# Start of a GRU with an expert layer: load requests on one queue, and two blocks of x turned in steps 0 and 1

## What is computed

```
gi = x_t @ W_ih + b_ih                     # 512 -> 3*512
gh = h @ W_hh + b_hh
r = sigmoid(i_r + h_r); z = sigmoid(i_z + h_z)
n = tanh(i_n + r * h_n)
h = (1 - z) * n + z * h                    # 256 such steps, one after the other

logits = h / |h| @ router_w                # top 2 of 8, weights normalized
out = x + sum_e combine[:, e] * (h @ Wa[e] @ Wb[e])
```

## Time and profile before

| | us |
|---|---|
| median of 3 runs | 1015.8 |
| lowest, highest | 1015.31, 1016.97 |
| the profiled execution | 1016.61 |
| its span in the profile | 1014.8 |
| granted TensorE clock, mean of the span | 0.998 |

### The profile page before, as it was taken

The page is one execution under the profiler, slowest core; times in us unless marked ns, Lnnn a source line. Parts: engine busy times, 40 slices in busy tenths (PEclk is TensorE's granted clock), DMA queues, the critical chain, the costliest instruction groups (busy, mean ns, idle before and its releaser), DMA issues.

```text
span 1014.8 us, 60727 instructions
## 1 busy us (share of the span) xinstructions
PE 979.8 (97%) x29067; PEld 669.7 (66%) x20799; DVE 877.1 (86%) x3637; ACT 695.7 (69%) x2696; POOL 292.5 (29%) x723
## 2 busy tenths in 40 slices
PE   4789999999999999999999999999999999999997
PEld 2456666666666667766666666666676677676674
DVE  6889888888888888888888888888888888888887
ACT  6687766776766776666677676677666667766664
POOL 1032233232333332323332332332332332233223
PEclk9999999999999999999999999999999999999999
DMA  8321111111111111111111111101111101110000
GB/s 294 94 81 30 30 32 30 26 31 31 28 32 30 28 29 33 27 32 33 28 26 35 27 31 30 32 24 34 30 29 30 33 23 34 30 30 20 14 9 28
DMA packets 49360, 38.83 MB, mean 38 GB/s; under 512 B 34532, under 2 KB 38972, under 8 KB 49084
## 3 DMA queue, kind: packets, MB, share of 16 engines
q1 hardware_dynamic: 48236, 31.41, 11.5%
q10 hardware_dynamic: 848, 3.54, 1.1%
HBM read 18.94 MB, written 8.39 MB: 27 GB/s over the span
## 4 chain that ended last, share of the span: by engine, by line
PE 90%; DVE 5%; DMA 2%; ACT 1%; issue 1%; SPq 0%; POOL 0%; DVEq 0%; POOLq 0%
PE pairs L872 16%; PE ybank L872 12%; PE gates L952 11%; PE gates L957 11%; PE pairs L863 8%; PE ybank L863 6%; PE zbank L872 5%; PE zbank L863 5%; PE obank L872 5%; PE nbank L872 5%; PE obank L863 3%; PE nbank L863 2%; DMA whh<-in_L_cond_W_hh 1%; DVE tr L737 1%; DVE acc L820 1%
## 5 line engine op out<-in xcount | busy, mean ns | idle before, releaser
L872 PE MATMUL pairs<-wx,xs 128*32 128x384 f16 x4096 | 280.8, 327 | 1.5 <-DVE wx L717 1.4
L599 ACT ACTIVATE rr<-pre 128x64 f32<-128x64 f32 x256 | 65.9, 258 | 239.8 <-DVE pre L740 239.8
L872 PE MATMUL ybank<-hparts,wa 128*128 128x128 f16 x2048 | 194.0, 219 | 0.0
L461 POOL TENSOR_TENSOR y<-y 128x128 f16<-128x128 f32 x256 | 106.4, 436 | 256.5 <-ACT y L650 251.9
L872 PEld LDWEIGHTS ybank<-hparts,wa 128*128 128x128 f16 x2048 | 159.9, 98 | 29.8 <-issue 16.7
L863 PE MATMUL ybank<-hparts,wa 128*128 128x128 f16 x1024 | 178.3, 219 | 0.0
L863 PE MATMUL pairs<-wx,xs 128*32 128x384 f16 x2048 | 174.1, 326 | 0.0
L952 PE MATMUL gates<-whh,st 128*32 128x256 f16 x4080 | 157.3, 273 | 15.4 <-DVE st L768 15.0
L872 PEld LDWEIGHTS pairs<-wx,xs 128*32 128x32 f16 x4096 | 108.3, 96 | 95.9 <-issue 54.1
L952 PEld LDWEIGHTS gates<-whh,st 128*32 128x32 f16 x4080 | 103.5, 96 | 84.7 <-ACT gates L571 62.6
L957 PE MATMUL gates<-whh,hparts 128*32 128x256 f16 x4080 | 157.5, 273 | 0.0
(11 more groups left out here) (138 smaller groups left out, 1820.9 us busy)
## 6 DMA issues: line engine op xcount, KB each, us to landing
out<-outb SPq DMA_DIRECT2D x63, 128.0 KB
xin<-in_x SPq DMA_DIRECT2D x58, 128.0 KB
wih<-in_L_cond_W_ih ACTq DMA_DIRECT2D x4, 768.0 KB, 7.9
whh<-in_L_cond_W_hh SPq DMA_DIRECT2D x4, 768.0 KB, 11.9
wih<-in_L_ffn_Wb SPq DMA_DIRECT2D x8, 256.0 KB, 2.6
xs<-xh SPq DMA_TRANSPOSE x116, 3.0
wih<-in_L_ffn_Wa SPq DMA_DIRECT2D x4, 256.0 KB, 5.0
whh<-in_L_ffn_Wa SPq DMA_DIRECT2D x4, 256.0 KB, 2.9
```

What stands on the lines that cost most here:

```text
L461: nc.gpsimd.tensor_tensor(y[:, m % YB, 1, :], y32[:, m % 2, :], y[:, m % YB, 0, :], ALU.subtract).then_inc(ylo_ready, 1)
L599: nc.scalar.activation(rr[:, :], pre[:, RG, :, :].rearrange("p k b -> p (k b)"), ACT.Sigmoid, scale=1 / PROD_SCALE).then_inc(r_ready, 1)
L872: return nc.tensor.matmul(out, lhsT, rhs, start=start, stop=stop, skip_group_check=True)
```

## The change

One queue, SP's, now requests W_ih parts 0 to 3, block 0 of x, W_hh parts 0 to 3, the router's weights, and blocks 1 and 2, in this order and without any wait between them. ScalarE requests the biases ahead of its splits, and `cond` behind split 2. Block 0's parts are made after split 11, not 8. Blocks 1 and 2 are turned by TensorE in steps 0 and 1 (ahead of the first state part and in step 0 before); their high parts are made by ScalarE in steps 0 and 1 (before: ahead of the steps, and in step 0), their low parts by VectorE in steps 1 and 2 (before: 0 and 1). The diff, with the same hunks in the order of the file:

```diff
@@ block.sync
-            sp.wait_ge(consts_ready, 2)
-            groups = "(g j c) -> j g c"
-            sp.dma_start(bias_h[0:P:32, HN, :], ...).then_inc(bias_loaded, 16)
-            sp.dma_start(bias_h[0:P:32, RG:ZG + 1, :], ...).then_inc(bias_loaded, 16)
-            sp.dma_start(bias_i[0:P:32, :, :], ...).then_inc(bias_loaded, 16)
-            for j in range(K):
-                sp.dma_start(cond_sb[32 * j:32 * j + B, :], cond[:, j * P:(j + 1) * P]).then_inc(cond_loaded, 16)
+            def load_ih(k):
+                sp.dma_start(wih32[:, k, :, :].rearrange("p g n -> p (g n)"), W_ih[k * P:(k + 1) * P, :]
+                             ).then_inc(wih_loaded[k], 16)
+
+            for k in range(K):
+                load_ih(k)
+            load_first(0)
             for k in range(K):
                 load_hh(k)
             sp.dma_start(rw32[:, :, :], router_w.rearrange("(p k) e -> p k e", k=K)).then_inc(rw_loaded, 16)
             for b in (1, 2):
-                sp.wait_ge(whh_loaded[b], 16)
                 load_first(b)
@@ block.scalar
-            for k in range(K):
-                if k == 2:
-                    act.dma_start(xin[:, 0, :], x_blocks[0]).then_inc(first_loaded[0], 16)
-                act.dma_start(wih32[:, k, :, :].rearrange("p g n -> p (g n)"), W_ih[k * P:(k + 1) * P, :]
-                              ).then_inc(wih_loaded[k], 16)
+            groups = "(g j c) -> j g c"
+
+            def load_biases():
+                act.wait_ge(consts_ready, 2)
+                act.dma_start(bias_h[0:P:32, HN, :], ...).then_inc(bias_loaded, 16)
+                act.dma_start(bias_h[0:P:32, RG:ZG + 1, :], ...).then_inc(bias_loaded, 16)
+                act.dma_start(bias_i[0:P:32, :, :], ...).then_inc(bias_loaded, 16)
+
+            def load_cond():
+                for j in range(K):
+                    act.dma_start(cond_sb[32 * j:32 * j + B, :], cond[:, j * P:(j + 1) * P]).then_inc(cond_loaded, 16)
+
@@ block.scalar, beside
-                if n == 0:
-                    split_first(2)
+                if n + 1 < FIRST:
+                    split_first(n + 1)
@@ block.scalar, the stream
             nc.scalar.activation(table_use[:, :], ones[:, :], ACT.Sigmoid)
+            load_biases()
             for n in range(N_GRU_SPLITS):
                 split_weights(n)
-                if n == 8:
+                if n == 2:
+                    load_cond()
+                if n == N_IH_SPLITS - 1:
                     split_first(0)
                 if n == N_IH_SPLITS:
                     keep_biases()
@@
-            split_first(1)
             for n in range(T):
@@ block.vector, beside
-                if n < FIRST - 1:
-                    split_first(n + 1)
+                if 1 <= n < FIRST:
+                    split_first(n)
@@ block.tensor, wide_step
                 pair_ahead(n)
+                if n == 1:
+                    turn_first(2)
@@ block.tensor, grouped_step
                 if n == 0:
-                    turn_first(2)
+                    turn_first(1)
@@ block.tensor, the stream
             pair_part(1, range(6))
-            turn_first(1)
             first_state_part()
```

More of the change, by code:

```diff
@@ L374, in beside @@
                     store(i - 2, s - 5)
-            sp.wait_ge(consts_ready, 2)
-            groups = "(g j c) -> j g c"
-            sp.dma_start(bias_h[0:P:32, HN, :], b_hh[2 * D:3 * D].rearrange("(j c) -> j c", j=K)).then_inc(bias_loaded, 16)
-            sp.dma_start(bias_h[0:P:32, RG:ZG + 1, :], b_hh[0:2 * D].rearrange(groups, g=2, j=K)).then_inc(bias_loaded, 16)
-            sp.dma_start(bias_i[0:P:32, :, :], b_ih.rearrange(groups, g=3, j=K)).then_inc(bias_loaded, 16)
-            for j in range(K):
-                sp.dma_start(cond_sb[32 * j:32 * j + B, :], cond[:, j * P:(j + 1) * P]).then_inc(cond_loaded, 16)
+            def load_ih(k):
[4 more added lines that the diff above has]
+            load_first(0)
             for k in range(K):
@@ L539, in _ @@
         def _(act):
-            for k in range(K):
-                if k == 2:
-                    act.dma_start(xin[:, 0, :], x_blocks[0]).then_inc(first_loaded[0], 16)
-                act.dma_start(wih32[:, k, :, :].rearrange("p g n -> p (g n)"), W_ih[k * P:(k + 1) * P, :]
-                              ).then_inc(wih_loaded[k], 16)
+            groups = "(g j c) -> j g c"
+            def load_biases():
+                act.wait_ge(consts_ready, 2)
+                act.dma_start(bias_h[0:P:32, HN, :], b_hh[2 * D:3 * D].rearrange("(j c) -> j c", j=K)).then_inc(bias_loaded, 16)
+                act.dma_start(bias_h[0:P:32, RG:ZG + 1, :], b_hh[0:2 * D].rearrange(groups, g=2, j=K)).then_inc(bias_loaded, 16)
+                act.dma_start(bias_i[0:P:32, :, :], b_ih.rearrange(groups, g=3, j=K)).then_inc(bias_loaded, 16)
+            def load_cond():
+                for j in range(K):
+                    act.dma_start(cond_sb[32 * j:32 * j + B, :], cond[:, j * P:(j + 1) * P]).then_inc(cond_loaded, 16)
             def split_weights(n):
```

## The result

| us | before | after |
|---|---|---|
| median of 10 runs each | 1015.92 | 1018.63 |
| lowest, highest | 1015.31, 1016.97 | 1017.80, 1019.99 |
| the profiled execution | 1016.61 | 1019.22 |
| its span | 1014.8 | 1017.4 |

The ratio is 1.0028, 95% interval 1.0019 to 1.0036: 2.7 us slower, between 1.9 and 3.7. The forecast was 1.1 slower, 1016.9, with a range from 1014.8 to 1019.2. The range held, with 0.6 to spare at its upper end. "Within 0.2%", with a chance of 0.77, did not come; "slower by over 2 us", with 0.18, did.

The account below looks back on a forecast made before the run. TensorE, busy 97%, bounds the kernel; the change only shifts the recurrence's start and adds work to steps. 0.5 + 0.6 = 1.1 later: 1017.7 against the profiled 1016.61, 1016.9 against the median 1015.8; range 1014.8 to 1019.2.

Parts of the forecast that it names:

- The loads, block 0 at 13.9: Start, SP's queue: block 0, now behind all of W_ih, lands at 13.9 instead of 10.08; bounds 12.2 and 14.4.
- W_ih complete at 11.6: Start, loads: all four W_ih parts are there at 11.6, where it was 15.78.
- The first rival: Start: block 0 lands early at 12.2, step 0's transpose at 26.1, time 1015.2; chance 0.20, of which 0.05 beyond 2 us.
- the 12.9: Start: block 0's landing if its copy takes an estimated 1.3 us by the skill's 207 GB/s; time then 1015.9.
- cond in time: Start: cond, requested by ScalarE from 7.1 to 9.0, lands at 15.9 and its state is ready at 17.1.
- The rival on the slower side: Start: cond is served only after all SP's requests, landing at 21.4; 4.2 later, 1020.0; chance 0.10.
- The bias chain, 5.2: TensorE, block 0's turning to biases: 5.2 as before, biases down at 19.1, sums kept 1.2 later.
- the slack of 2.6: Before the change, ScalarE keeps the bias sums at 17.88, 2.6 us after they are there; the change spends this.
- Step 0's gates 0.5 later: VectorE, step 0's first gates transpose: about 27.8 instead of 27.25, 0.5 later; prediction wrong if before 26 or after 29.
- Steps 0 to 2: Moved turning and splits: steps 0 and 1 covered by idle time, step 2 on full VectorE 0.6 later, bounds 0 and 0.65.
- The clock rival: TensorE's biases and state part all at the lower clock: 2.0 on top, 1018.9 to 1019.2; chance 0.08.
- The sum: Whole kernel: 0.5 ahead of step 0 plus 0.6 in step 2, 1.1 later.

Follow-up runs that it names:

- loads_only: The kernel after with its loads, but blocks 1 and 2 turned and split where the kernel before has them: 1018.11, ratio to before 1.0018.
- fill_state: The kernel after with 15 unused matmuls in the first state part, five ahead of each wait for W_hh 1 to 3: 1018.15, ratio to before 1.0025.
- fill_start: The kernel after with 40 unused transposes of the identity on TensorE ahead of the wait for block 0: 1018.22, ratio to before 1.0021.
- turn_only: The kernel before, loads untouched, with only the turning and splits of blocks 1 and 2 moved as in the change: 1016.56, ratio 1.0006.
- late_splits: Kernel after; block 0 requested between W_ih 1 and 2, cond turned behind split 8, router's and experts' low parts one step later: 1025.99, ratio to before 1.0093.
- turn_inside: The kernel before with block 1 turned inside the first state part, ahead of the wait for W_hh's last low part: 1016.76, ratio 1.0008.

## Why the prediction was right, and where it was off

- **The loads, block 0 at 13.9.** 14.49 in the profile after, 13.94, 14.01 and 13.74 in loads_only, fill_state and fill_start, where TensorE also waits for it in this queue order. W_ih complete at 11.6: split from 11.89. The count of bytes ahead, with the lag of the same request, was good to 0.6. The first rival (block 0 at 12.2) did not come; the measured landings are 0.8 to 1.6 later than the 12.9 that came out with the figure for rows 512 KiB apart of the Trainium skill ("DMA: Bandwidth & Descriptors", section "Latency and other measured facts").
- **cond in time.** The state was ready at 18.38, ahead of its copy at 20.64; cond had landed 6.1 after its requests (the median of the four). The rival on the slower side did not come. That ScalarE would stand still for 1.9 us while it issues the cond requests was wrong: split 3 started at 7.02, 0.26 after the end of the ones before, when its part landed. ScalarE's table load came at 0.72, not 1.9. So W_ih's last part was split from 11.89, after a wait of 1.41, and not from 12.3 with hardly any wait.
- **The bias chain, 5.2.** 14.49 to 20.22 are 5.7, and with block 0's 0.6 the sums were kept 2.37 later, not 1.2; these two terms, too small by 0.5 and 0.6, are the largest error of the sum. The same turning and bias matmuls took 5.2 to 6.9 in kernels that differ in nothing near them (before 5.2, after 5.7, loads_only 6.1, turn_only 6.9), 3.7 after filler. The third bias call alone took 1.02, 1.22, 1.59 and 1.91 in these four, from about the full clock's length to about the lower one's. I took one execution's length as a constant; it hangs on when the clock rises. Before the change the slack of 2.6 hid this: turn_only's biases ended 1.5 later than the kernel before's, and its sums were kept at the same time.
- **Step 0's gates 0.5 later: 1.68.** All of the difference is in the two terms above. The hand-over behind the last split took 0.4, as said, and the turning taken away was worth 0.7, as turn_only shows. The transpose at 28.93 was 0.07 short of the 29 from which the prediction called itself wrong.
- **Steps 0 to 2.** Step 2: 0.6 expected, 0.46 measured, shown by late_splits. Step 0 was costed at nothing, covered by "over 1 us idle": at the lower clock the cover is gone, 0.46, shown by fill_state. The clock rival had the low clock in the biases and the state part and priced it at 2.0; it cost 0.5 in the biases, and behind the state part, where nobody had it, 0.5 more.
- **The sum.** 1.1 expected, 2.6 in the span: 1.2 more ahead of step 0, 0.46 in step 0, 0.14 less in step 2, 0.16 in step 12. Step 12 is the loads' doing: it takes 4.48 to 4.50 in all ten kernels that have the loads on one queue and the splits in their places, and 4.32 to 4.33 in the kernel before, turn_only and turn_inside. By what way is open.
- **What was luck.** The path up to step 0 and the loss in step 2 were as forecast, but the losses in steps 0 and 12 were not, and the errors of size nearly all went the same way. The change costs two and a half times the forecast, and the time is inside the range because its upper end had been drawn for the lower clock, not because the sum was good.

## What to carry to other kernels

A load moved up on a queue moves another one down, and the one that waits longest is often not the one with the most bytes: here the weights came 4 us sooner for nothing, because the small block behind them starts a serial chain through TensorE, ScalarE and VectorE. Before spending a slack, ask how much the work behind it varies, not only how long it was once. And cover by "idle time of TensorE" is worth its length only at the clock that TensorE has at that point.

## What the runs showed that was not expected

- The clock in the first stretches of these traces is not to be trusted: those at 13 to 18 us say 1.00, while the turning matmuls at 14.49 took 1.09, as those at 30.61 under a granted 0.50 (1.12), and not the 0.66 of the full clock.
- ScalarE can issue DMAs while its activations run: four cond requests, which stand behind the third split in its stream, went out from 5.11 to 6.98 beside three splits from 5.10 to 6.76.
- The time around the span is 1.75 to 1.9 us in every execution of twelve kernels and the kernel before, and 1.77 to 3.62 in the nine of fill_start.
